# A tuned two-block transformer kernel on one core: TensorE's tile slots brought to 768 instructions each, with 256-column passes and waits that are already met

## Chip, cores and metric

The kernel runs on one core of a Trainium2 chip. The metric is the device time of one execution in microseconds (us); lower is better. In the text PE is TensorE (PEld its weight loads), DVE is VectorE, ACT is ScalarE, POOL is GpSimd and SP is SyncE, which issues the DMAs.

## The reference, cut to what matters

The input is four sequences of 512 tokens with 128 features. Two adaptive-norm blocks follow. The first has a 16-head ALiBi attention and a mixture of eight experts. The second has a 4-head attention with a memory term, and then a small transformer of six layers, which is where the change lies:

```python
for i in range(DEPTH):            # DEPTH = 6, x: 4 x 512 x 128
    x = attn_layer(shift_tokens(x), Wqkv[i], q_scale[i], k_scale[i], Wo[i]) + x
    x = ffn_layer(shift_tokens(x), ln_g[i], ln_b[i], W1[i], b1[i], W2[i], b2[i]) + x
# attn_layer: qkv = x @ Wqkv (128 x 3072); q, k normalised and rotated;
#   16 heads of 64, windows of 32 queries on 64 keys; softmax; @ V; @ Wo (1024 x 128)
# ffn_layer: layernorm; a, gate = split(xn @ W1 + b1); (a * gelu(gate)) @ W2 + b2
```

## The kernel before, in words

Each engine has its own hand-written instruction stream, and semaphores join them. Until about 690 us the kernel computes the first block and the attention of the second. Then comes the **tile stage**: `run_slots` (L443) calls the engine's `slot` function 96 times, for 6 layers x 4 sequences x 4 tiles of 128 tokens (t = 0 to 3). The number of a slot is g. A slot is software-pipelined: it projects its own tile g, and does the window attention of g-1 and g-2 and parts of the feed-forward network of sequences before it. `drain` (L1285) finishes what is left.

On TensorE a slot (`slot`, L1127) runs in this order, which is the order of the code:

- `queries(0)`: a projection (`project`, L1036) onto 512 of the 3072 columns. It has three passes in float32r, since x and W are split into high and low parts: high x high, high x low, low x high. They accumulate in `pj`.
- `wo_quarter` (L1179): the output projection of one tile, 8 float32 products of 128x128 on `wo`. The trace shows two passes for each float32 product.
- for t = 3 a norm's transposes (`norm_in`), then `queries(1)`, the second projection; for t = 3 also `ff_down` (L1187).
- `probs` (L1152): 8 transposes of softmax weights; then `project(.., 2)`.
- `values_(0)` (L1161): 32 small products of 64x32 on `slab` (V2) into `oo`; then `project(.., 3)`.
- `turn_k` (L1145): 16 transposes; then `values_(1)`, 32 more small products, and `project(.., 4)`.
- `window_scores(.., 0)` (L1085): 32 small products into `sc`.
- `out_` (L1172): 16 transposes of the attention's result (`tr<-ident,slab`). They wait for DVE's `weighted`.
- for t < 3 `ff_up` (L1117): one third of the first feed-forward product, 6 passes of float32r in two accumulation groups. For t = 3 `norm_back` instead, 4 transposes.
- `window_scores(.., 1)`, `turn_q` (16 transposes) and `project(.., 5)`.

Each product is two instructions in TensorE's stream, a weight load (LDWEIGHTS) and a MATMUL. A float32 product that is no transposition is four, because of its two passes. Further semaphore waits than the one that an instruction carries itself are instructions of their own, and one of these holds up to two waits. Counted so, a slot has 713 to 717 instructions for t < 3, and 733 or 734 for t = 3. The whole stream has 76,612: twice 37,572, and 1,468 wait instructions. No instruction of this kernel is in a loop; the stream is straight.

Of the kernel before, what the change touches and what calls it, by code (L numbers as in the profile page):

```python
# [15 lines left out]
P = 128  # L16
B = 4
S = 512
# [78 lines left out]
        self.eng.wait_ge(self.sem, self.base + self.n)  # L97

PTR = 6
NMAX = 2 * H0 * T
# [7 lines left out]
def build(nc, ins, out):  # L110
    ctx = ExitStack()
    with ctx:
# [52 lines left out]
        w1_lo = nc.alloc_sbuf_tensor_at("w1_lo", [P, 2 * DI], F32R, offset=w1_at)  # L165
# [11 lines left out]
        hB_hi = nc.alloc_sbuf_tensor_at("hB_hi", [P, S], F32R, offset=xcur_at + 4 * S)  # L177
        hT_at = here()
        hT = sb("hT", [P, 2, S])
        hB_lo = nc.alloc_sbuf_tensor_at("hB_lo", [P, S], F32R, offset=hT_at)  # L180
        xs_lo = nc.alloc_sbuf_tensor_at("xs_lo", [P, S], F32R, offset=hT_at + 4 * S)
# [4 lines left out]
        xs_hi = sb("xs_hi", [P, S], F32R)  # L186
# [85 lines left out]
        def rows(b):  # L272
# [15 lines left out]
        spare = a.take(3, INNER)  # L288
# [6 lines left out]
        w1_hi = nc.alloc_sbuf_tensor_at("w1_hi", [P, 2 * DI], F32R, offset=arena_at + 4 * a.at)  # L295
# [15 lines left out]
        pj = ctx.enter_context(nc.psum_tensor("pj", [P, 2, S], F32))  # L311
# [9 lines left out]
        ld_const = sem("ld_const")  # L321
        ld_late = sem("ld_late")
# [34 lines left out]
        pj_mm, sq_ev, rot_ev, ss_ok, qk_rdy, v_cp = (  # L357
            sem("pj_mm"), sem("sq_ev"), sem("rot_ev"), sem("ss_ok"), sem("qk_rdy"), sem("v_cp"))
# [8 lines left out]
        ld_w1, w1_h, w1_l, hb_h, hb_l = sem("ld_w1"), sem("w1_h"), sem("w1_l"), sem("hb_h"), sem("hb_l")  # L367
# [247 lines left out]
        n_const, n_mid, n_late = (16 * N_CONST.count(k) for k in range(3))  # L615
# [12 lines left out]
        def _(pe):  # L628
            def mm(o, l, r, start=True, stop=True, **k):
                return nc.tensor.matmul(o, l, r, start=start, stop=stop, **k)  # L630
# [35 lines left out]
            for g in range(2):  # L666
                for k in range(4):
                    last = tp(tr[:, g, k * P:(k + 1) * P], wnat[:, 4 * g + k, :])
# [367 lines left out]
            def project(g, t, c):  # L1036

                low_, high_ = W_LO[g // (T * B) % 2], W_HI[g // (T * B) % 2]
                if c < 2:
                    wait(pe, v_cp, g * 2 - 1 + c)  # L1040
                else:
                    pe.wait_ge(rot_ev, g * 4 + c - 1)
                x_, w_ = slice(t * P, (t + 1) * P), slice(c % 2 * S, (c % 2 + 1) * S)
                k = c // 2
                mm(pj[:, c % 2], xs_hi[:, x_], high_[k][:, w_], stop=False)
                mm(pj[:, c % 2], xs_hi[:, x_], low_[:, k, w_], start=False, stop=False)
                mm(pj[:, c % 2], xs_lo[:, x_], high_[k][:, w_], start=False).then_inc(pj_mm, 1)

            def turn_rows(rows, done, ready, first, second):

# [66 lines left out]
            def ff_up(m, k, bank):  # L1117
                w = CH[k][1]
                for half, o in ((1, DI + CH[k][0]), (0, CH[k][0])):
                    mm(bank[0:w, half], w1_hi[:, o:o + w], hB_hi[:, :], stop=False)  # L1120
                    mm(bank[0:w, half], w1_lo[:, o:o + w], hB_hi[:, :], start=False, stop=False)
                    if half:
                        pe.wait_ge(hb_l, m + 1)
                    last = mm(bank[0:w, half], w1_hi[:, o:o + w], hB_lo[:, :], start=False)
                last.then_inc(w1_mm, 1)

            def slot(s_):  # L1127
                l, b, t, n, g = s_.l, s_.b, s_.t, s_.n, s_.g
                new, c_, d_, m1, m2 = s_.new, s_.c_, s_.d_, s_.m1, s_.m2
                n2, t2 = (n, t - 2) if t >= 2 else (n - 1, t + 2)  # L1130
                weighted_ = min(g - 2, NTILE)

                def queries(c):
                    if c == 0 and t < 2:
                        pe.wait_ge(xs_l, n * 2 + t + 1)
                    project(g, t, c)
# [42 lines left out]
                def wo_quarter(m, i):  # L1179
                    pe.wait_ge(o_cp, (m * T + i + 1) * 2)  # L1180
                    tok, held = slice(i * P, (i + 1) * P), slice(i % 2 * P, (i % 2 + 1) * P)
                    for p_ in range(PAIRS):
                        last = mm(oo[:, 1, tok], wo[:, p_, :], oT[:, p_, held], start=(p_ == 0),
                                  stop=(p_ == PAIRS - 1))
                    last.then_inc(wo_mm, 1)
# [11 lines left out]
                if b == 0 and t == 0:  # L1197
                    pe.wait_ge(wl_ok[0], l + 1)
                queries(0)
                if s_.mw is not None:  # L1200
                    if b == 0 and t == 3:
                        pe.wait_ge(ld_wo, (l + 1) * G * 16)
                    if 1 <= t < 3 and m2 is not None:
                        pe.wait_ge(up_cp, m2 * 4 + 2 * t - 1)
                    if t == 3 and m2 is not None:
                        pe.wait_ge(gelu_ev, gated(m2, 2))
                    wait(pe, on_ok, g * 2 - 4)
                    wo_quarter(s_.mw, s_.iw)
                if t == 3 and m1 is not None:
                    pe.wait_ge(t_sub, g - 1)  # L1210
                    pe.wait_ge(xs_part, m1 * T + T)
                    norm_in(LNB, LNB_BANKS[0], xsF)
                queries(1)
                if g > 0:
                    crossing(g, 1)
                if g == 1:
# [1327 lines left out]
```

## Time and profile before

| | us |
|---|---|
| median of 3 runs | 2113.81 (2111.32 to 2116.18) |
| the profiled execution's own time | 2119.18 |
| its span in the trace | 2117.4 |
| PE busy / DVE busy / ACT busy / POOL busy | 1943.4 / 1821.4 / 1546.8 / 1290.5 |
| tile stage, slots 8 to 94 (87 slots) | 1357.18 |

The span is what the trace covers; the execution's own time has some 1.8 us around it. "Busy" is the time in which an engine has an instruction at work. The rows further down are from this one execution. In a timeline row "x64" is a number of MATMULs in a row (two for each of the 32 small products), and "[1.09 <-issue]" is idle time ahead of the row and what ended it: the engine that was waited for, or "issue" where the profile sees nothing that was waited for. In the rows 64*32 is the loaded weight, and a small product's output is 32x64.

### The profile page before, as it was taken

To read this page: it belongs to the slowest core of one execution; us is meant where nothing else is said; L and a number is where in the kernel's file an instruction comes from. 1 tells how busy PE (TensorE), PEld (TensorE's weight loads), DVE (VectorE), ACT (ScalarE), POOL (GpSimd) and SP (SyncE) were. 2 spreads that over 40 slices of the span, in tenths; PEclk is the share of its full clock that TensorE was granted. 3 is DMA by queue.
4 is the path that set the end of the run, shared out by engine and by line. 5 is a ranking of instruction groups with operands and counts; after the bars stand their busy time and mean duration, and the time that the engine had idled before them with its cause. 6 is when DMAs were issued, how large, how long until landed. Compare 5 with 4: busy or idle time off the path is not lost.

```text
span 2117.4 us, 89360 instructions
## 1 busy us (share of the span) xinstructions
PE 1943.4 (92%) x37572; PEld 1442.3 (68%) x37572; DVE 1821.4 (86%) x3995; ACT 1546.8 (73%) x3028; POOL 1290.5 (61%) x1551
## 2 busy tenths in 40 slices
PE   6888899987788999999999999999999999999996
PEld 4666664455566777777777777777777777777774
DVE  6788775577798999999899999999999998998994
ACT  4777763355576877888788887888878878777873
POOL 1111110000378888788787888878888887777771
PEclk9999999998899999999999999999999999999998
DMA  5000000100232322332333323333233332222321
GB/s 117 2 2 2 2 32 31 61 1 1 58 86 70 79 68 70 93 84 67 78 83 78 87 65 77 86 89 79 67 81 83 87 75 63 73 75 73 77 63 41
DMA packets 99377, 132.62 MB, mean 63 GB/s; under 512 B 29052, under 2 KB 44034, under 8 KB 98978
## 3 DMA queue, kind: packets, MB, share of 16 engines
q1 hardware_dynamic: 98978, 126.90, 23.6%
q8 instruction: 299, 4.90, 1.0%
q14 instruction: 100, 0.82, 0.1%
HBM read 28.20 MB, written 1.11 MB: 14 GB/s over the span
## 4 chain that ended last, share of the span: by engine, by line
PE 48%; DVE 23%; ACT 10%; issue 9%; SPq 5%; POOL 3%; DMA 2%; DVEq 0%; POOLq 0%; ACTq 0%
PE pj L630 15%; PE oo L630 15%; ACT arena L1961 7%; PE sc L630 6%; PE tr L1057 5%; DVE arena L1764 4%; DVE arena L1766 4%; SPq L555 3%; PE tr L633 3%; DMA slab<-arena 2%; DVE bv L1772 2%; DVE arena L1521 2%; DVE small L1795 1%; DVE xn L1353 1%; ACT L1965 1%
## 5 line engine op out<-in xcount | busy, mean ns | idle before, releaser
L1961 ACT ACTIVATE arena<-tr 128x512 f32<-128x512 f32 (+3 forms) x894 | 458.8, 562 | 100.0 <-PE tr L633 51.3
L2397 POOL TENSOR_TENSOR arena<-arena 128x1024 f32<-128x1024 f32 x192 | 457.4, 2382 | 91.3 <-DVE arena L1766 87.5
L1961 ACT ACTIVATE arena<-pj 128x512 f32<-128x512 f32 x576 | 332.5, 599 | 150.9 <-PE pj L630 96.1
L2415 POOL TENSOR_TENSOR arena<-arena,small 128x1024 f32<-128x1024 f32 x192 | 365.6, 1904 | 28.1 <-POOL small L2408 0.9
L1961 ACT ACTIVATE arena<-arena 128x1024 f32<-128x1024 f32 (+4 forms) x446 | 304.6, 693 | 87.6 <-DVE arena L1521 74.0
L1772 DVE TENSOR_REDUCE bv<-arena 128x8 f32<-128x512 f32 x384 | 252.7, 679 | 2.9
L630 PE MATMUL oo<-slab,arena 64*32 64x64 f32 (+1 forms) x12416 | 232.7, 229 | 10.5 <-issue 9.7
L2364 POOL TENSOR_SCALAR rstd<-mv 128x4 f32<-128x4 f32 x40 | 11.4, 284 | 364.5 <-DVE mv L1347 364.4
L633 PE MATMUL tr<-ident,arena 128*128 128x128 f32 x1346 | 206.4, 280 | 19.4 <-DMA beta<-in_L_attn_betas 9.9
L630 PEld LDWEIGHTS oo<-slab,arena 64*32 64x32 f32 (+1 forms) x12416 | 160.8, 106 | 80.0 <-issue 44.4
L633 PEld LDWEIGHTS tr<-ident,arena 128*128 128x128 f32 x1346 | 163.3, 143 | 58.3 <-issue 23.9
L630 PEld LDWEIGHTS sc<-arena 64*32 64x32 f32 x12288 | 136.1, 105 | 87.6 <-issue 71.9
L630 PEld LDWEIGHTS oo<-arena,wo 128*128 128x128 f32 x1504 | 183.6, 193 | 8.7 <-DMA wo<-in_L_ffn_Wo 0.3
L630 PE MATMUL sc<-arena 64*32 64x64 f32 x12288 | 171.7, 224 | 18.4 <-issue 17.5
L630 PE MATMUL oo<-arena,wo 128*128 128x128 f32 x1504 | 184.4, 276 | 0.0
L1785 DVE TENSOR_REDUCE small<-sc 128x16 f32<-128x1024 f32 x96 | 117.3, 1222 | 46.9 <-PE sc L630 46.9
L1764 DVE TENSOR_TENSOR arena<-pj,rtab 128x512 f32<-128x512 f32 x192 | 131.3, 684 | 29.3 <-ACT arena L1961 27.3
L1057 PEld LDWEIGHTS tr<-ident,arena 64*128 64x128 f32 x3072 | 111.3, 139 | 63.0 <-issue 42.1
L1057 PE MATMUL tr<-ident,arena 64*128 64x64 f32 x3072 | 138.0, 229 | 16.6 <-ACT arena L1961 9.3
L1764 DVE TENSOR_TENSOR arena<-pj,wT 128x512 f32<-128x512 f32 x192 | 131.2, 684 | 22.0 <-ACT arena L1961 19.3
L1809 DVE TENSOR_TENSOR slab<-oo,small 128x512 f32<-128x512 f32 x192 | 123.7, 686 | 12.1 <-PE oo L630 8.7
L1766 DVE TENSOR_TENSOR arena<-pj,wT 128x512 f32<-128x512 f32 x192 | 130.8, 681 | 0.0
(340 smaller groups left out, 4465.0 us busy)
## 6 DMA issues: line engine op xcount, KB each, us to landing
slab<-arena SPq DMA_DIRECT2D x576, 128.0 KB
slab<-arena SPq DMA_DIRECT2D x336, 64.0 KB
arena<-gate_mem SPq DMA_DIRECT2D x24, 256.0 KB, 4.4
wqkv<-in_L_ffn_Wqkv SPq DMA_DIRECT2D x36, 128.0 KB, 2.5
arena<-in_L_ffn_Wqkv SPq DMA_DIRECT2D x36, 128.0 KB, 2.3
wo<-in_L_ffn_Wo SPq DMA_DIRECT2D x24, 128.0 KB, 2.5
w<-in_L_ffn_W SPq DMA_DIRECT2D x6, 341.0 KB, 3.6
YT<-in_L_attn_x SPq DMA_DIRECT2D x4, 256.0 KB, 3.9
```

The lines of the kernel that those rows point to most:

```text
L555: sp.dma_start(V2[u * DL:(u + 1) * DL, t % 2, w, :], Vt[(w - 1) * WIN:(w + 1) * WIN, t % 2, f]).then_inc(v2_in[t % 2], 16)
L630: return nc.tensor.matmul(o, l, r, start=start, stop=stop, **k)
L633: return nc.tensor.transpose(o, i, ident[0:i.shape[0], 0:i.shape[0]])
L1057: last = nc.tensor.transpose(tr[:, u, pr * DL:(pr + 1) * DL], rows(r, pr), ident[r, r])
L1764: v.tensor_tensor(ra[:, t % 2, k, co].rearrange("p (h u d) -> p h u d", u=2, d=DL // 2), src, tc_.unsqueeze(1).broadcast_to(wide), ALU.mult)
L1766: v.tensor_tensor(rb[:, k, co].rearrange("p (h u d) -> p h u d", u=2, d=DL // 2), src[:, :, ::-1, :], ts_.unsqueeze(1).broadcast_to(wide), ...
L1772: v.tensor_reduce(ss[:, k, hf * PAIRS:(hf + 1) * PAIRS, 0], sq[:, c % 2].rearrange("p (h d) -> p h d", d=DL), AX.X, ALU.add).then_inc(ss_o ...
L1785: v.tensor_reduce(mx, s_v, AX.X, ALU.max).then_inc(mx_ok, 1)
L1809: v.tensor_tensor(On.rearrange("p (a u d) -> p u a d", u=2, d=DL)[:, :, a_], oo[:, :, :].rearrange("p u (a d) -> p u a d", d=DL)[:, :, a_] ...
L1961: return nc.scalar.activation(o, i, f, **k)
L2397: p_.tensor_tensor(r_, r_, rb[:, k, :], ALU.add).then_inc(sum_ok, 1)
L2415: p_.tensor_tensor(r3, r3, rs[:, k, :].unsqueeze(2).broadcast_to([P, HL, DL]), ALU.mult).then_inc(qk_rdy, 1)
```

## The change

Only TensorE's stream changes, and only in the tile stage. The streams of the other engines hold the same instructions in the same order. Three things are done:

1. `project` runs its three passes over 256 columns instead of 512 for c = 0, 1, 2 and 5, twice over. That is 12 more load-and-product pairs in a slot. `ff_up` does the same for its tokens, 6 more pairs in each slot with t < 3, and its first group waits for `hb_l` in both halves.
2. `spread_out` adds wait instructions on `ld_const` and `ld_late`, semaphores of the loads at the kernel's start. The same stream has already waited for both values before the tile stage. A slot gets 17, 19, 19 or 10 of them (t = 0 to 3), in three groups: behind `queries(0)`, behind `wo_quarter` and behind `queries(1)`.
3. Slots 0 to 7 have numbers of their own (0, 0, 0, 0, 8, 43, 43, 24), which sets where in the stream the count of 256 begins anew inside the slots that follow.

```diff
+SPARE_AT = (17, 19, 19, 10)
+SPARE = {0: 0, 1: 0, 2: 0, 3: 0, 4: 8, 5: 43, 6: 43, 7: 24}
...
-                mm(pj[:, c % 2], xs_hi[:, x_], high_[k][:, w_], stop=False)
-                mm(pj[:, c % 2], xs_hi[:, x_], low_[:, k, w_], start=False, stop=False)
-                mm(pj[:, c % 2], xs_lo[:, x_], high_[k][:, w_], start=False).then_inc(pj_mm, 1)
+                x_, k, n = slice(t * P, (t + 1) * P), c // 2, S // (2 if c in (0, 1, 2, 5) else 1)
+                parts = [(slice(o, o + n), slice(c % 2 * S + o, c % 2 * S + o + n)) for o in range(0, S, n)]
+                for o_, w_ in parts:
+                    mm(pj[:, c % 2, o_], xs_hi[:, x_], high_[k][:, w_], stop=False)
+                    mm(pj[:, c % 2, o_], xs_hi[:, x_], low_[:, k, w_], start=False, stop=False)
+                    last = mm(pj[:, c % 2, o_], xs_lo[:, x_], high_[k][:, w_], start=False)
+                last.then_inc(pj_mm, 1)
...
+                    tok = [slice(u * S // 2, (u + 1) * S // 2) for u in range(2)]
+                    for u in tok:
+                        mm(bank[0:w, half, u], w1_hi[:, o:o + w], hB_hi[:, u], stop=False)
+                        mm(bank[0:w, half, u], w1_lo[:, o:o + w], hB_hi[:, u], start=False, stop=False)
+                        if half:
+                            pe.wait_ge(hb_l, m + 1)
+                        last = mm(bank[0:w, half, u], w1_hi[:, o:o + w], hB_lo[:, u], start=False)
...
+            def spread_out(n):
+                for _ in range(n):
+                    pe.wait_ge(ld_const, n_const)
+                    pe.wait_ge(ld_late, n_late)
...
+                spare = SPARE.get(g, SPARE_AT[t])
...
                 queries(0)
+                spread_out(spare // 3)
...
                     wo_quarter(s_.mw, s_.iw)
+                spread_out(spare // 3)
...
                 queries(1)
+                spread_out(spare - spare // 3 * 2)
```

Every slot from g = 8 on then has 768 instructions on TensorE (one of 767 or 770 stands where a layer's weights change), and the stream 81,328 in all.

The start of a slot with t = 0 on PE, in the program before, from `queries(0)` to `queries(1)` (`wq_hi` is the high part of the query weights, `w_lo` the low part, the suffix B the second buffer):

```order
L630 MATMUL pj<-wq_hiB,xs_hi 128x512 [waits v_cp,xs_l]
L630 MATMUL pj<-w_loB,xs_hi 128x512
L630 MATMUL pj<-wq_hiB,xs_lo 128x512
L630 MATMUL oo<-arena,wo 128x128 [waits o_cp,on_ok]
L630 MATMUL oo<-arena,wo 128x128 x7
L630 MATMUL pj<-wq_hiB,xs_hi 128x512 [waits v_cp]
L630 MATMUL pj<-w_loB,xs_hi 128x512
L630 MATMUL pj<-wq_hiB,xs_lo 128x512
```

The same place in the changed program:

```order
L633 MATMUL pj<-wq_hiB,xs_hi 128x256 [waits v_cp,xs_l]
L633 MATMUL pj<-w_loB,xs_hi 128x256
L633 MATMUL pj<-wq_hiB,xs_lo 128x256
L633 MATMUL pj<-wq_hiB,xs_hi 128x256
L633 MATMUL pj<-w_loB,xs_hi 128x256
L633 MATMUL pj<-wq_hiB,xs_lo 128x256
L633 MATMUL oo<-arena,wo 128x128 [waits ld_const,ld_late,on_ok,o_cp]
L633 MATMUL oo<-arena,wo 128x128 x7
L633 MATMUL pj<-wq_hiB,xs_hi 128x256 [waits ld_const,ld_late,v_cp]
```

Each projection has six products instead of three, and the added waits stand between it and `wo_quarter`, and again before the next projection. The places of the other products have not moved.

The feed-forward part of a slot with t < 3 on PE, before; the row behind it is the second half of the window scores:

```order
L630 MATMUL oo<-hB_hi,w_hi 128x512 [waits on_ok,hb_h]
L630 MATMUL oo<-hB_hi,w_lo 128x512
L630 MATMUL oo<-hB_lo,w_hi 128x512 [waits hb_l]
L630 MATMUL oo<-hB_hi,w_hi 128x512
L630 MATMUL oo<-hB_hi,w_lo 128x512
L630 MATMUL oo<-hB_lo,w_hi 128x512
L630 MATMUL sc<-arena 32x64 x32
```

And the first six of its twelve rows in the changed program (six more without waits follow, then the same row of window scores):

```order
L633 MATMUL oo<-hB_hi,w_hi 128x256 [waits on_ok,hb_h,w1_l]
L633 MATMUL oo<-hB_hi,w_lo 128x256
L633 MATMUL oo<-hB_lo,w_hi 128x256 [waits hb_l]
L633 MATMUL oo<-hB_hi,w_hi 128x256
L633 MATMUL oo<-hB_hi,w_lo 128x256
L633 MATMUL oo<-hB_lo,w_hi 128x256 [waits hb_l]
```

Twelve products of half the width stand in the place of six.

## Rows read from the trace of the kernel before

**Rows 1.** The page: TensorE's busy line, and the queue that brings instructions.

```profile
PE 1943.4 (92%) x37572; PEld 1442.3 (68%) x37572; DVE 1821.4 (86%) x3995; ACT 1546.8 (73%) x3028; POOL 1290.5 (61%) x1551
...
q8 instruction: 299, 4.90, 1.0%
```

**Rows 2.** Windows: slots 8 to 94 together, then three single slots (columns in the first row).

```profile
core 0: us, PE busy (x) PEld busy (x) DVE busy (x) ACT busy (x) POOL busy (x), PEclk, DMA share, GB/s
689.79:2046.97 1357.18, 1304.21 (x30794) 1011.40 (x30792) 1250.43 (x2296) 1102.40 (x2081) 1101.18 (x1302) 1.00 0.31 77
1066.50:1081.03 14.53, 14.40 (x354) 11.31 (x353) 13.99 (x25) 12.84 (x26) 11.43 (x15) 1.00 0.41 100
...
1468.93:1483.46 14.53, 14.53 (x353) 11.36 (x352) 13.51 (x24) 13.20 (x23) 12.16 (x16) 1.00 0.32 77
1111.66:1128.74 17.08, 16.48 (x362) 12.37 (x360) 16.71 (x37) 12.45 (x26) 12.56 (x16) 1.00 0.28 72
```

**Rows 3.** Waits of PE from 700 to 2060 us: total, times, longest.

```profile
PE sc L630 <- issue: 12.9, 17, 1.4
PE tr L1057 <- DVE slab L1809: 8.9, 18, 1.4
PE tr L1057 <- ACT arena L1961: 8.4, 13, 1.3
```

**Rows 4.** Timeline of PE in the first half of a slot's window scores.

```profile
1011.03 0.64 PE L630 MATMUL sc<-arena 64*32 64x64 f32 x38
1012.76 0.43 PE L630 MATMUL sc<-arena 64*32 64x64 f32 x26 [1.09 <-issue]
```

**Rows 5.** Windows from one such break to two later ones (columns as in rows 2).

```profile
1012.70:1028.98 16.28, 14.65 (x378) 11.77 (x378) 14.11 (x26) 12.08 (x25) 13.45 (x16) 1.00 0.25 60
1012.70:1090.76 78.06, 74.09 (x1765) 57.83 (x1764) 70.57 (x130) 62.32 (x120) 63.68 (x75) 1.00 0.29 72
```

**Rows 6.** Windows of five single stretches of 256 instructions.

```profile
1102.94:1106.56 3.62, 2.53 (x133) 1.86 (x130) 3.58 (x8) 3.56 (x8) 3.23 (x9) 1.00 0.52 146
...
1007.80:1012.75 4.95, 3.87 (x130) 2.72 (x125) 4.92 (x9) 3.95 (x8) 3.45 (x6) 1.00 0.51 123
996.93:1000.33 3.40, 2.88 (x141) 2.29 (x138) 3.33 (x8) 1.90 (x5) 3.25 (x4) 1.00 0.02 5
1071.20:1075.14 3.94, 3.86 (x148) 2.71 (x134) 3.90 (x8) 3.33 (x7) 2.39 (x1) 1.00 0.65 156
1075.14:1078.84 3.70, 3.65 (x137) 2.82 (x141) 3.67 (x7) 3.08 (x7) 3.10 (x6) 1.00 0.09 22
```

**Rows 7.** Timeline of PE at the window scores of a slot with t = 3.

```profile
996.81 0.86 PE L630 MATMUL sc<-arena 64*32 64x64 f32 x64
998.14 0.97 PE L1057 MATMUL tr<-ident,slab 64*128 64x64 f32 x16 [0.47 <-DVE slab L1809]
...
999.63 1.02 PE L630 MATMUL sc<-arena 64*32 64x64 f32 x64
```

**Rows 8.** Timeline of PE: 512-column passes of `ff_up`, and `wo_quarter`.

```profile
1887.38 0.39 PE L630 MATMUL oo<-hB_hi,w_hi 128*128 128x512 f32 x1
1887.61 0.40 PE L630 MATMUL oo<-hB_hi,w_lo 128*128 128x512 f32 x1
...
1892.31 1.95 PE L630 MATMUL oo<-arena,wo 128*128 128x128 f32 x16
1894.02 0.47 PE L630 MATMUL pj<-wq_hiB,xs_hi 128*128 128x512 f32 x1
```

**Rows 9.** Timeline of PE in the first block: float32r passes of 256 and 384 columns.

```profile
185.80 0.37 PE L630 MATMUL pj<-Kst,Qm 128*128 128x256 f32 x1
186.00 0.38 PE L633 MATMUL tr<-ident,arena 128*128 128x128 f32 x2
186.14 0.42 PE L630 MATMUL sc<-Kst,Qm 128*128 128x384 f32 x1
186.41 0.49 PE L633 MATMUL tr<-ident,arena 128*128 128x128 f32 x3
```

More of the change, by code:

```diff
@@ L1042, in project @@
                     pe.wait_ge(rot_ev, g * 4 + c - 1)
-                x_, w_ = slice(t * P, (t + 1) * P), slice(c % 2 * S, (c % 2 + 1) * S)
-                k = c // 2
-                mm(pj[:, c % 2], xs_hi[:, x_], high_[k][:, w_], stop=False)
-                mm(pj[:, c % 2], xs_hi[:, x_], low_[:, k, w_], start=False, stop=False)
-                mm(pj[:, c % 2], xs_lo[:, x_], high_[k][:, w_], start=False).then_inc(pj_mm, 1)
+                x_, k, n = slice(t * P, (t + 1) * P), c // 2, S // (2 if c in (0, 1, 2, 5) else 1)
[5 more added lines that the diff above has]
+                last.then_inc(pj_mm, 1)
             def turn_rows(rows, done, ready, first, second):
@@ L1119, in ff_up @@
                 for half, o in ((1, DI + CH[k][0]), (0, CH[k][0])):
[L1120 to L1124, printed above, removed]
+                    tok = [slice(u * S // 2, (u + 1) * S // 2) for u in range(2)]
[5 more added lines that the diff above has]
+                        last = mm(bank[0:w, half, u], w1_hi[:, o:o + w], hB_lo[:, u], start=False)
                 last.then_inc(w1_mm, 1)
+            def spread_out(n):
+                for _ in range(n):
+                    pe.wait_ge(ld_const, n_const)
+                    pe.wait_ge(ld_late, n_late)
             def slot(s_):
```

## The prediction, as it was put on record

> **What bounds the kernel now.** I read the page first. PE is the busiest engine at 92%, with DVE behind it at 86% [rows 1]. Then I cut out the tile stage, the only part that the change touches: in 87 slots of it PE is busy for 1304.2 of 1357.2 us, at a granted clock of 1.00, and DVE for 1250.4 [rows 2]. So PE is the bound there, and all of its idle time is 53.0 us. A slot takes 1357.18 / 87 = 15.60 us.
>
> Third, the waits. The three longest groups of them stand ahead of the small products and transposes, and the first is put down to "issue": nothing that the profile sees was waited for [rows 3]. The timeline shows one of these breaks. It falls inside 64 equal passes of window scores, behind the 38th, and lasts 1.09 us; no semaphore stands there [rows 4].
>
> Fourth, the counts. From this break to the next one at 1028.98 there are 378 products, so 756 instructions, and 12 waits by the program: 768, three times 256. To a break inside another group of scores at 1090.76 there are 1765 products, so 3530, and 54 waits: 3584, 14 times 256 [rows 5]. And the queue that brings instructions moved 299 packets of 4.90 MB [rows 1], 16.4 KB each, for the 76,612 instructions of PE's stream: 256.2 to a packet. So PE's instructions come in **pieces of 256**, and the breaks are at the starts of pieces.
>
> Last, how long a piece needs. I counted on from 1012.76 and read stretches of 256 instructions. One that holds only small products, one projection and scores has 2.53 us of work and took 3.62; another with 3.87 took 4.95. Two others with nearly 4 us of work, 3.94 and 3.70, took what their work takes [rows 6]. My reading: the next piece is called for only around the start of the one before, and a piece can't take less than some 3.4 to 4 us, now and then 5. A piece with a projection or two lasts longer and hides this; one of mostly small products doesn't. Slots have 713 to 734 instructions, so the starts of pieces wander through them, and every few slots a short piece comes up.
>
> One text speaks against this reading. The Trainium skill, "Runtime: NRT & Kernel Launch", section "Instruction fetch mechanics", also has blocks of 16 KiB or 256 instructions, but says that the fetch is "hidden by the ~20-cyc/instr NX issue floor". By that the breaks would have another cause and placing the starts would save nothing; that is the third rival below. The break of rows 4 speaks against it.
>
> **The change, part by part.** The sum is made against the profiled execution, 2119.18 us (span 2117.4), 5.4 us over the median.
>
> *Removed: wandering starts.* Undisturbed slots with t < 3 take 14.53 us, and with t = 3 17.08 [rows 2]. Four of them take 3 x 14.53 + 17.08 = 60.67, or 15.17 a slot. What short pieces cost now is 15.60 - 15.17 = 0.43 a slot, times 87: **37 us**. The undisturbed slots hold the real waits for DVE and ACT; those remain.
>
> *Added: fixed starts.* With 768 in each slot, a slot always has three starts at the same places. Counted on through the changed stream, which is the same up to the tile stage, they are:
> - in `values_(0)` (19th of its 32 products; 15th for t = 3),
> - early in the first half of the window scores (8th; 4th for t = 3),
> - late in the second half (25th).
>
> Piece A, from values to scores, holds two projections, a turn and 45 small products. Its like in the trace is the stretch at 1071.20: 3.94 us for 3.86 of work [rows 6], 0.05 lost at the most likely.
>
> Piece B, from scores to scores, holds `out_` and for t < 3 `ff_up`. Its like is the stretch at 1075.14: 3.70, with 3.65 of work [rows 6]. In the changed stream `ff_up` has 12 instructions more, so B ends some 3 products sooner, at about 3.55 of work. Against a need of 3.4 to 4 that loses between 0 and 0.45; I take 0.1, near the low end, since the stretch at 1075.14 went by in 3.70.
>
> For t = 3 B has no `ff_up`. From 996.9 it holds the rest of the scores, 0.47 of waiting for DVE, 16 transposes, 4 more and 25 small products, some 2.9 us in all; the second half of the scores then took 1.02 where 0.86 is the rule, a start of a piece with little delay [rows 7]. The stretch from 996.93, which begins and ends near the same products, took 3.40 [rows 6]. So this loses from 0.16, the delay in rows 7, to 1.1 at a need of 4; I take 0.45, to the 3.4 of the like stretch.
>
> Piece C is the rest, 7 us or more, and loses nothing. Four slots lose 3 x (0.05 + 0.1) + 0.05 + 0.45 = 0.95 us; 87 / 4 x 0.95 = **21 us** come back. The gain by placement is 37 - 21 = 16.
>
> *Added: more passes.* There are 12 more in each slot and 6 more for t < 3, so 66 in four slots. A 512-column pass follows the last after 0.23 [rows 8]. A 256-column pass was followed after 0.20 by the transposes, a 384-column pass after 0.27 [rows 9], so 128 columns are worth about 0.06 to 0.07, and four times 0.0575 is the 0.23. The pass costs by its columns, with hardly a fixed part, if the load of its weights is hidden. Behind 128 columns in float32, 16 loads and passes took 1.71 us from start to start, 0.107 each [rows 8], so a load is done within 0.107 and fits behind a pass of 0.115. I take 2 ns for each added pass: 66 x 0.002 x 87 / 4 = **3 us**. Bounds: nothing, since the columns are the same; and 5 ns, since rounding hides that much, 7 us. That the load isn't hidden is excluded by the 0.107.
>
> *Added: met waits.* 65 in four slots, 1430 in all. They are queued behind a projection (0.69 us of passes) or `wo_quarter` (1.71), ahead of work that isn't waited for soonest, and PE's queue takes what is issued ahead. Rows 8 show `wo_quarter` with two waits ahead of it and the projection behind it, one more wait, with no break. So **0**. If that cover were gone, as after a projection that was itself late, each would cost what it takes to issue; no row has that. Slots 5 and 6 have 14 or 15 in a group, and there I allow 1 us once. Upper bound: 0.1 us a slot, 9 us.
>
> DVE's order is not changed. It needs 1250.4 of the 1357.2 us [rows 2], so it would become the bound only at 106 us saved.
>
> Sum: 2119.2 - 37 + 21 + 3 + 1 = 2107, which is 12 less; against the median of 2113.8 that is **2102**.
>
> **The rivals.**
>
> *Short pieces are slower than I take them (slower).* If a piece that begins in the scores always needs 4.0 us, each B loses 0.45 for t < 3 and 1.1 for t = 3: 4 x 0.05 + 3 x 0.45 + 1.1 = 2.65 in four slots. 58 us come back, and with 4 for passes and waits the kernel takes 2113.8 - 37 + 58 + 4 = 2139. The point from which it decides: 33 us may come back, 1.5 in four slots, 1.3 of it in B; 3 x (need - 3.55) + (need - 2.9) = 1.3 gives a need of 3.7 in every B. For: 4.95. Against: 3.62, 3.40, and 3.70 with hardly a break [rows 6]. Chance 0.17, mostly with a need little over that point, 2118 to 2130.
>
> *All is hidden (much faster).* B lasts long enough for t < 3, and for t = 3 its start falls into the wait for DVE. Then 37 is gained and 4 lost: 2081. For: 0.16 of delay in rows 7. Against: the spread in rows 6. Chance 0.13.
>
> *The breaks are no fetches (no change).* Then only passes and waits are added: 2114 + 4 = 2118, or with waits that cost nothing 2114. For: two of the three longest groups are put down to DVE and ACT, 17.3 us [rows 3]. Against: breaks 256 apart. The same time results if PE, no longer held at starts, waits for DVE's `weighted` instead. Chance 0.15. (The section of the Trainium skill named above would make this the likeliest.)
>
> **How the numbers follow.** The forecast case has 0.55: 2102, from 2090 to 2113. A measurement of this kernel can tell 0.2%, 4.2 us, from no change. Faster (under 2109.6): 0.50 of the forecast case and 0.13, 0.63. Same: 0.05 and 0.15, 0.20. Slower: 0.17. The range for 8 in 10 leaves out the far ends on both sides: 2084 to 2121.
>
> **What would show it.** In the profile after: 318 packets in the instruction queue; slots of 768 instructions whose breaks all stand behind the same product, in scores or not at all; slots with t < 3 near 14.7 and nearly equal; t = 3 at 17.4 to 17.7; passes of 256 columns 0.115 to 0.12 apart; no idle time ahead of `wo_quarter` and `queries(1)`. It is wrong if t < 3 slots take over 15.1, if breaks stand in the second half of scores in most slots, or if 256-column passes are 0.13 or more apart.

## The result, and the profile after

The changed kernel takes 2099.1 us (median of 6 runs, 2091.14 to 2105.65). The kernel before took 2112.57 beside it on the same chip (6 runs, 2105.12 to 2116.18). The ratio is **0.994**, 95% interval 0.9914 to 0.9968. The forecast was 2102. The profiled execution took 2105.65, with a span of 2103.9.

The page of the changed kernel, first part and queues, against [rows 1]:

```profile
PE 1957.8 (93%) x39156; PEld 1558.3 (74%) x39156; DVE 1820.7 (87%) x3995; ACT 1547.0 (74%) x3028; POOL 1290.6 (61%) x1551
...
q8 instruction: 317, 5.19, 1.0%
```

Windows of the changed kernel (columns as in rows 2): slots 8 to 94, then three single slots, of which the second has t = 3, then slots 0 to 7, slot 7 alone, and all that follows slot 94:

```profile
697.38:2031.72 1334.34, 1309.04 (x32234) 1109.49 (x32233) 1249.73 (x2296) 1102.33 (x2082) 1100.54 (x1302) 1.00 0.31 79
1498.09:1512.66 14.57, 14.53 (x372) 12.67 (x371) 14.02 (x24) 12.66 (x25) 11.50 (x14) 1.00 0.31 75
1541.81:1559.01 17.20, 16.54 (x375) 13.11 (x373) 16.61 (x38) 11.89 (x26) 13.84 (x17) 1.00 0.26 64
1189.70:1205.46 15.76, 14.71 (x372) 12.70 (x371) 14.56 (x24) 12.15 (x25) 14.21 (x16) 1.00 0.32 78
564.55:697.38 132.83, 106.82 (x2401) 89.45 (x2399) 113.08 (x211) 82.76 (x164) 95.31 (x116) 0.88 0.27 69
678.15:697.38 19.23, 17.34 (x368) 14.89 (x367) 15.59 (x35) 13.01 (x26) 13.27 (x16) 0.76 0.25 64
2031.72:2103.90 72.18, 55.73 (x957) 44.38 (x955) 42.73 (x78) 29.35 (x51) 19.60 (x24) 0.86 0.17 45
```

The same of the kernel before, where they did not stand in rows 2: slots 0 to 7, slot 7, and what follows slot 94:

```profile
563.37:689.79 126.42, 100.22 (x2303) 76.86 (x2302) 112.94 (x211) 82.26 (x164) 94.53 (x116) 0.95 0.28 72
672.36:689.79 17.43, 14.07 (x355) 11.20 (x354) 16.22 (x36) 13.24 (x26) 12.80 (x17) 1.00 0.28 71
2046.97:2117.40 70.43, 52.90 (x911) 38.02 (x909) 42.31 (x78) 29.58 (x51) 19.60 (x24) 0.92 0.18 47
```

Waits of PE from 700 us on in the changed kernel, against [rows 3]:

```profile
PE tr L1062 <- DVE slab L1826: 10.0, 21, 0.5
PE tr L1062 <- ACT arena L1978: 7.8, 8, 1.1
...
PE sc L633 <- issue: 0.7, 3, 0.3
```

Rows 3 show one group that ends in "issue". The kernel before has three more of them in the same stretch, which the changed kernel doesn't have at all:

```profile
PE oo L630 <- issue: 7.7, 15, 0.9
PE tr L1057 <- issue: 4.6, 6, 1.5
...
PE pj L630 <- issue: 1.4, 3, 0.5
```

What there is to see:

- **The waits that nothing explained are gone.** "issue" was 26.6 us in all, 12.9 of it ahead of the scores, and is 0.7. The waits for DVE and ACT, which are real, stayed (8.9 and 8.4 before, 10.0 and 7.8 now). PE's idle time in the 87 slots fell from 53.0 to 1334.34 - 1309.04 = 25.3 us.
- **Most slots are now the same.** They take 14.57 us, or 17.20 for t = 3; the means over the windows are 14.76, 14.60, 14.85 and 17.23 (t = 0 to 3). The slot at 1189.70 is one of the few that don't, and its break is a real wait, the first row below.
- **The time went into two places that the prediction left out.** The 87 slots gained 22.8 us, but slots 0 to 7 lost 6.4 and the part behind slot 94 lost 1.8. In both the granted clock is lower: 0.88 for 0.95, and 0.86 for 0.92. In slots 0 to 7 PE's busy time rose by 106.82 - 100.22 = 6.6 us, and its idle time stayed at 26.

Timeline of PE in the changed kernel: the break in the slot at 1189.70, two 256-column passes at 2.4 GHz, and two in slot 2:

```profile
1203.41 0.71 PE L1062 MATMUL tr<-ident,arena 64*128 64x64 f32 x16 [1.01 <-ACT arena L1978]
...
1500.23 0.29 PE L633 MATMUL pj<-wq_hiB,xs_lo 128*128 128x256 f32 x1
1500.35 0.28 PE L633 MATMUL pj<-wq_hiB,xs_hi 128*128 128x256 f32 x1
...
601.91 0.41 PE L633 MATMUL pj<-w_lo,xs_hi 128*128 128x256 f32 x1
602.12 0.41 PE L633 MATMUL pj<-wq_hi,xs_lo 128*128 128x256 f32 x1
```

A pass is followed after 0.12 us in a full slot and after 0.21 in slot 2, whose granted clock is 0.81. The second is the lower level, 1.2 GHz.

| stretch | before | after | difference |
|---|---|---|---|
| up to slot 0 | 563.37 | 564.55 | +1.2 |
| slots 0 to 7 | 126.42 | 132.83 | +6.4 |
| slots 8 to 94 | 1357.18 | 1334.34 | -22.8 |
| behind slot 94 | 70.43 | 72.18 | +1.8 |
| span | 2117.4 | 2103.9 | -13.5 |

Each column is one execution. A second profile of the changed kernel (e11 below) has 563.16, 132.60, 1337.89 and 72.35, so that slots 8 to 94 gain 19.3 us there, and the first row shows no difference.

### The profile page after: what moved, and what is told of

Read it like the earlier page. It is cut to its first block, busy times and chain, and to the rows that moved or that the text cites. A ratio compares the mean times of both kernels' runs of the same rounds, so it can differ in the third digit from the quotient of the medians.

```text
span 2103.9 us, 94076 instructions
## 1 busy us (share of the span) xinstructions
PE 1957.8 (93%) x39156; PEld 1558.3 (74%) x39156; DVE 1820.7 (87%) x3995; ACT 1547.0 (74%) x3028; POOL 1290.6 (61%) x1551
## 4 chain that ended last, share of the span: by engine, by line
PE 57%; DVE 19%; ACT 10%; issue 7%; SPq 3%; POOL 2%; DMA 2%; DVEq 0%; POOLq 0%; ACTq 0%
PE pj L633 19%; PE oo L633 19%; ACT arena L1978 7%; PE tr L1062 6%; PE sc L633 6%; PE tr L636 4%; DVE arena L1781 3%; DVE arena L1783 2%; ACT L1982 2%; SPq L558 2%; DVE xn L1370 2%; DVE arena L1538 2%; DMA slab<-arena 1%; PE oo L636 1%; DVE small L1812 1%
## 5 line engine op out<-in xcount | busy, mean ns | idle before, releaser
L633 PE MATMUL oo<-slab,arena 64*32 64x64 f32 (+1 forms) x12416 | 227.7, 229 | 2.5 <-issue 1.8
L633 PEld LDWEIGHTS oo<-arena,wo 128*128 128x128 f32 x1504 | 177.4, 193 | 0.5 <-issue 0.2
L633 PE MATMUL pj<-w_lo,xs_hi 128*128 128x256 f32 (+1 forms) x480 | 148.8, 310 | 0.0
L1781 DVE TENSOR_TENSOR arena<-pj,wT 128x512 f32<-128x512 f32 x192 | 131.1, 683 | 19.4 <-ACT arena L1978 18.3
L633 PE MATMUL pj<-w_loB,xs_hi 128*128 128x256 f32 (+1 forms) x480 | 145.8, 304 | 0.0
```

Of the source, the lines that this page charges most:

```text
L1781: v.tensor_tensor(ra[:, t % 2, k, co].rearrange("p (h u d) -> p h u d", u=2, d=DL // 2), src, tc_.unsqueeze(1).broadcast_to(wide), ALU.mult)
```

## The experiments

All diffs are against the changed kernel. **Where the starts stand** is given as a number x: the first start of a slot stands x instructions behind the last pass of `queries(0)`, the others 256 and 512 further on. In the change x is 168. The wait of `values_(0)` for `v2_*` and `pt_cp`, at which PE's sequencer really stands in each slot (for 1.1 to 3 us, an estimate from the timelines), is instruction 91 (t = 0), 93 (t = 1 and 2) or 107 (t = 3) by the same count. The numbers for slots 4 to 7 set x for the rest of the stage. Slot times by t are means over the slots' windows unless a single slot is named.

| kernel | x | waits a slot | slots 8 to 94 | ratio to before (95%) |
|---|---|---|---|---|
| the change | 168 | 10 to 19 | 1334.3 | 0.9941 (0.9914 to 0.9968) |
| e11_change_again | 168 | 10 to 19 | 1337.9 | 0.9937 (0.9918 to 0.9956) |
| e3_early_shift | 168 | 10 to 19 | 1339.8 | 0.9936 (0.9916 to 0.9956) |
| e7_starts_earlier | 153 | 10 to 19 | 1336.5 | 0.9943 (0.9925 to 0.9962) |
| e9_late_passes | 158 | 10 to 19 | 1339.0 | 0.9933 (0.9910 to 0.9956) |
| e6_starts_later | 217 | 10 to 19 | 1345.8 | 1.0010 (0.9993 to 1.0027) |
| e4_passes_only | wanders | 0 | 1361.9 | 1.0024 (1.0011 to 1.0037) |
| e10_one_group | 168 | 10 to 19, together | 1391.7 | 1.0169 (1.0133 to 1.0204) |
| e1_other_starts | 8 | 10 to 19 | 1397.2 | 1.0220 (1.0194 to 1.0247) |
| e2_best_starts | 64 | 10 to 19 | 1393.2 | 1.0240 (1.0212 to 1.0268) |
| e8_wait_47_in | 44 | 10 to 19 | 1388.7 | 1.0273 (1.0251 to 1.0295) |
| e5_waits_only | 192 | 34 to 55 | 1448.8 | 1.0470 (1.0444 to 1.0497) |

### e1_other_starts

```diff
-SPARE = {0: 0, 1: 0, 2: 0, 3: 0, 4: 8, 5: 43, 6: 43, 7: 24}
+SPARE = {0: 0, 1: 0, 2: 0, 3: 0, 4: 6, 5: 6, 6: 5, 7: 5}
```

> The changed kernel with 22 instead of 118 added waits in slots 4 to 7, all else the same. Each slot from g = 8 on still has 768 instructions of the same kinds in the same order, but the piece of 256 begins 160 instructions earlier in it: in wo_quarter, in turn_k and in out_. Placement theory: read off the changed kernel's own timeline, the stretch between the second and third start has about 2.3 us of work where some 3.6 are needed, so four slots lose 4.8 us and 88 slots about 105; less 4 us for the fewer waits: 2099 + 100 = 2199, ratio to the kernel before 1.035 to 1.055, slots with t < 3 near 15.8. Rival (the narrower passes and the waits do it, wherever pieces begin): no slower than the change, 2095 to 2100, ratio 0.992 to 0.995. Rival (DVE and ACT set the time): the same 2095 to 2100.

It took 2163.36 us, ratio 1.022. Slots 8 to 94 in the windows, and the largest group of PE's waits from 700 us on:

```profile
691.49:2088.67 1397.18, 1318.95 (x32234) 1118.76 (x32233) 1251.03 (x2296) 1109.24 (x2083) 1104.51 (x1303) 0.99 0.30 75
...
PE sc L633 <- issue: 69.3, 75, 1.6
```

The same instructions, in the same order from slot 8 on; only the place in them where a piece of 256 begins is another. The group that went from 12.9 to 0.7 in the change is now 69.3: a break or two in nearly every slot with t < 3, and none to speak of for t = 3, which took 17.19. So **the place of the starts alone is worth 63 us between the best and a bad choice**, and the breaks are the starts of pieces. Counted through the streams, all 75 breaks over 0.4 us that end in "issue" in this stretch of e1 open a piece of 256; so do all 31 such breaks of the kernel before, and of the 25 breaks over 0.4 us that it owes to DVE or ACT one does. The 63 us are some 0.6 of the loss that was expected.

### e2_best_starts

```diff
-SPARE = {0: 0, 1: 0, 2: 0, 3: 0, 4: 8, 5: 43, 6: 43, 7: 24}
+SPARE = {0: 0, 1: 0, 2: 0, 3: 0}
...
+            for _ in range(314):
+                pe.wait_ge(ld_x[0], 16)
```

The loop stands at the start of PE's program and gives 157 instructions, two waits in each.

> The changed kernel with its slots' pieces beginning 104 instructions earlier in the slot than in the change (about 64 behind the end of queries(0)), and the 118 waits of slots 4 to 7 replaced by the usual 17, 19, 19, 10; the rest of the shift, 157 waits, stands at the start of the program, where PE waits for the first loads for about 10 us anyway. By the changed kernel's timeline every piece then holds 4.1 us of work or more. Placement theory: no piece breaks at all, slots 14.56 and 17.2, which is 15.22 on average against 15.34 (10 us), and slots 4 to 7 give back 5 to 6 us: 2084 to 2088, ratio 0.985 to 0.990. If starts are not what costs: 2093, by the slots 4 to 7 alone, or 2099 if the early waits cost what those did.

A clear miss: 2167.55 us, ratio 1.024, although by their work no piece is short. Two things went wrong. The first is in the timeline of PE at the start of the program, e2:

```profile
20.99 1.94 PE L636 MATMUL tr<-ident,arena 128*128 128x128 f32 x8 [20.99 <-issue]
```

The kernel before:

```profile
9.87 1.97 PE L633 MATMUL tr<-ident,arena 128*128 128x128 f32 x8 [9.87 <-DMA beta<-in_L_attn_betas]
```

157 waits that are already met hold PE up by 11.1 us. The first of them is taken at some 4.1, when the load of x has landed, so each takes (20.99 - 4.1) / 157 = 0.108 us. e8, with 20 more of them in the same place, needs no such reading: it starts at 23.21, which is 0.111 us for each of the 20.

```profile
23.21 1.94 PE L636 MATMUL tr<-ident,arena 128*128 128x128 f32 x8 [23.21 <-issue]
```

 **A met wait isn't free; it takes PE's sequencer some 0.11 us.**

The second is in every slot. Timeline of PE in e2, a slot with t = 3 (from 1519.10), and under it ACT, whose first copy of `tr` is what `values_(0)` waits for:

```profile
1528.72 0.41 PE L633 MATMUL oo<-slab,arena 64*32 64x64 f32 x21
1530.09 0.68 PE L633 MATMUL oo<-slab,arena 64*32 64x64 f32 x43 [0.95 <-issue]
...
1525.36 1.09 ACT L1980 ACTIVATE arena<-tr 128x512 f32<-128x512 f32 x2 [1.42 <-PE tr L636]
```

PE has done the piece's last product at 1529.14 and goes on at 1530.09. The piece had begun at 1522.05, behind the last pass of `queries(1)`: 8.0 us, where the longest of rows 6 took 4.95. The DMA view tells why. From 1522.00 to 1527.20 the queues moved this:

```profile
DMA packets 589, 0.92 MB, mean 177 GB/s; under 512 B 139, under 2 KB 139, under 8 KB 589
q1 hardware_dynamic: 589, 0.92, 69.7%
```

And from 1527.20 to 1527.40:

```profile
q8 instruction: 1, 0.02, 47.3%
```

In the first 5.2 us of the piece no packet of instructions moves at all. The packet with the next piece comes at 1527.2, 1.2 us after the wait of `values_(0)` was met (1526.0), and 2.8 us later PE goes on. Of the 22 slots of e2 with t = 3, 15 show this, with the packet 1.1 to 1.7 us after the wait was met; in the other 7 the packet came 3.2 to 3.3 us before it, which stays unexplained. So the next piece isn't called for at the start of the one before, as the prediction had it, but some way into it, and a wait that really holds the sequencer in between delays the call by all that it takes. In e2 this wait is 27 or 29 instructions behind a start (43 for t = 3); in the change 179 or 181 (195).

### e3_early_shift

```diff
-SPARE = {0: 0, 1: 0, 2: 0, 3: 0, 4: 8, 5: 43, 6: 43, 7: 24}
+SPARE = {0: 0, 1: 0, 2: 0, 3: 0}
...
+            for _ in range(106):
+                pe.wait_ge(ld_x[0], 16)
```

> The change with the starts of pieces exactly where the change has them, but reached by 53 waits at the start of the program and the usual 65 in slots 4 to 7. All theories: equal to the change but for slots 4 to 7, which are 5 to 6 us shorter: 2093 to 2094, ratio 0.990 to 0.992. If the 86 waits in slots 5 and 6 are free, as the prediction had it to within 1 us: 2098, ratio 0.994.

2104.76 us, ratio 0.9936: not to be told from the change, and not the 0.990 to 0.992 that was expected. The 53 waits stand where PE waits for a load anyway (its first product starts at 10.12 instead of 9.87). Slots 0 to 7 took 130.8 us, 2 less than in the change, and not the 126.4 of before: so it isn't mainly the 53 extra waits in slots 4 to 7 that slow the filling.

### e4_passes_only

```diff
             def spread_out(n):
+                n = 0
 
                 for _ in range(n):
```

> The narrower passes without any added wait: 749 or 751 instructions in a slot, 758 for t = 3, so the starts wander again, by 18 or so a slot. Placement theory: about as slow as the kernel before, since wandering starts cost 30 to 45 us in 88 slots, plus 3 us for the passes: 2112 to 2120, ratio 1.000 to 1.004. Rival (the narrower passes themselves give the gain): 2099, ratio 0.994.

2123.09 us, ratio 1.0024. Slots 8 to 94:

```profile
693.72:2055.57 1361.85, 1314.11 (x32234) 1112.55 (x32233) 1250.40 (x2296) 1105.21 (x2083) 1102.46 (x1303) 1.00 0.31 77
```

The 256-column passes bring nothing by themselves. PE is busy for 9.9 us more than before and the stretch is 4.7 longer, and the starts wander as before: "issue" is 28.6 us in all, for 26.6 before. The gain is the placement's.

### e5_waits_only

```diff
-SPARE_AT = (17, 19, 19, 10)
-SPARE = {0: 0, 1: 0, 2: 0, 3: 0, 4: 8, 5: 43, 6: 43, 7: 24}
+SPARE_AT = (53, 55, 55, 34)
+SPARE = {0: 0, 1: 0, 2: 0, 3: 0, 4: 9, 5: 9, 6: 9, 7: 9}
...
-                x_, k, n = slice(t * P, (t + 1) * P), c // 2, S // (2 if c in (0, 1, 2, 5) else 1)
+                x_, k, n = slice(t * P, (t + 1) * P), c // 2, S
...
-                    tok = [slice(u * S // 2, (u + 1) * S // 2) for u in range(2)]
+                    tok = [slice(0, S)]
```

> The change without its 256-column passes: the products are those of the kernel before, and the 768 of a slot are filled up with met waits alone (53, 55, 55, 34 a slot; 9 in each of slots 4 to 7), so that the pieces begin behind the same products as in the change. If it is the places of the starts that save the time and a met wait costs nothing, slots with t < 3 take 14.5 to 14.7, and the ratio to before is 0.988 to 0.996, like the change's 0.994. If the shorter passes had a part in the gain, it is 0.996 to 1.003. If a met wait costs 3 ns or more, the 197 a period of four slots add 0.6 us and more, and the ratio is 1.000 and up.

2213.32 us, ratio 1.047, the worst of all. The largest waits of PE in the tile stage:

```profile
PE tr L636 <- issue: 76.4, 61, 1.3
PE oo L633 <- issue: 20.6, 21, 1.1
```

And the timeline of PE in a slot with t = 1, at two of the three groups of 18 or 19 waits:

```profile
1506.09 0.39 PE L633 MATMUL pj<-wq_hiB,xs_lo 128*128 128x512 f32 x1
1507.40 2.02 PE L633 MATMUL oo<-arena,wo 128*128 128x128 f32 x16 [0.93 <-issue]
...
1510.00 0.39 PE L633 MATMUL pj<-wq_hiB,xs_lo 128*128 128x512 f32 x1
1511.64 1.06 PE L636 MATMUL tr<-ident,arena 128*128 128x128 f32 x8 [1.25 <-issue]
```

The starts are quiet: scores lose 4.9 us to "issue" in the whole stage. The time is lost at the waits, in gaps of 0.9 to 1.3 us behind each projection. 18 waits at 0.11 are 2 us, and what PE still has queued covers the rest. So the third answer of the expectation holds, and the "3 ns" in it was far too low a bound: 132 waits more in four slots cost 114.5 us in 87, or 40 ns each on the average. With so many waits this run can't show what the starts alone would bring without the narrower passes.

### e6_starts_later and e7_starts_earlier

```diff
-SPARE = {0: 0, 1: 0, 2: 0, 3: 0, 4: 8, 5: 43, 6: 43, 7: 24}
+SPARE = {0: 0, 1: 0, 2: 0, 3: 0, 4: 17, 5: 17, 6: 17, 7: 18}
```

> The change with all three starts 49 instructions later in each slot (17, 17, 17, 18 waits in slots 4 to 7), so that the wait of values_(0) for DVE stands some 130 instructions behind a start and the scores are begun at other places. If only the work between two starts counts (need 3.6 us), no piece is short at all, t = 3 takes under 17.2 and the ratio is 0.985 to 0.992. If a piece is called for only when PE's sequencer is some 40 to 56 instructions into the one before, the delays of those first instructions count too, every slot breaks once by 0.5 to 1.1 us, and the ratio is 1.005 to 1.025.

```diff
-SPARE = {0: 0, 1: 0, 2: 0, 3: 0, 4: 8, 5: 43, 6: 43, 7: 24}
+SPARE = {0: 0, 1: 0, 2: 0, 3: 0, 4: 12, 5: 48, 6: 48, 7: 25}
```

> The change with all three starts 15 instructions earlier (12, 48, 48, 25 waits in slots 4 to 7). Both theories, the one by the work between starts and the one by the call 40 to 56 instructions in, leave at most 0.6 us lost in four slots: ratio 0.989 to 0.997, slots with t < 3 near 14.6. If starts in values_(0) are good only at the very place of the change, it is over 1.0.

e7 came out as both theories had it: 2102.19 us, ratio 0.9943, t < 3 at 14.66 to 14.89. The place has some 15 instructions of room on that side. e6 gave 2116.37, ratio 1.001, between the two expectations. Its waits of PE:

```profile
PE sc L633 <- issue: 8.8, 13, 1.1
...
PE tr L1062 <- issue: 7.2, 14, 1.0
```

It breaks in some slots and not in others, 27 times in 87 slots: t = 3 takes 17.63, where the change has 17.23, t = 2 15.0, t = 0 and 1 14.74 and 14.61. A theory that counts only the work between two starts is refuted, since by it e6 is the best place of all. The other had the direction and not the size: at least 1.005.

### e8_wait_47_in

```diff
-SPARE = {0: 0, 1: 0, 2: 0, 3: 0, 4: 8, 5: 43, 6: 43, 7: 24}
+SPARE = {0: 0, 1: 0, 2: 0, 3: 0}
...
+            for _ in range(354):
+                pe.wait_ge(ld_x[0], 16)
```

> As e2_best_starts, with 20 more waits at the start of the program: the starts are 20 instructions earlier, and the wait of values_(0) for DVE stands 47 instructions into its piece instead of 27 (62 and 42 for t = 3). By the work between the starts this is worse than e2: some 1.2 us lost in four slots where that theory gives e2 nothing; e2 lost 3.2. If the call for the next piece is made about 40 instructions in, the wait no longer holds it up: under 1.5 us lost in four slots, slots with t < 3 at 14.6 to 15.0, ratio 0.995 to 1.010. If it is made about 56 in, it does: 2.5 to 3.5 lost, ratio 1.018 to 1.030.

2172.04 us, ratio 1.027. In e8 the wait is 47 instructions behind a start for t = 0, 49 for t = 1 and 2, and 63 for t = 3. The slots took 16.16, then 15.09 and 15.52, then 17.13. Against the change's undisturbed 14.57 and 17.20 that is 1.6 us lost, then 0.5 and 0.95, then nothing. The ratio and these 3 us in four slots are what was expected if the call is made about 56 in; but that t = 3 loses nothing at 63, and that t = 1 and 2 lose less than t = 0, narrows it from both sides. In e2, with the wait 43 in, t = 3 took 17.71. The windows of the same slot with t = 3, e2:

```profile
1519.10:1537.30 18.20, 16.42 (x374) 13.13 (x373) 17.35 (x38) 13.12 (x26) 12.88 (x19) 1.00 0.25 61
```

And e8, with its `values_(1)` in the timeline, in which e2 broke for 0.95 us:

```profile
1520.72:1537.82 17.10, 16.56 (x374) 13.18 (x373) 16.66 (x38) 12.43 (x26) 12.27 (x16) 1.00 0.26 65
...
1530.34 0.86 PE L633 MATMUL oo<-slab,arena 64*32 64x64 f32 x64
1531.27 0.50 PE L633 MATMUL pj<-wv_hiB,xs_hi 128*128 128x512 f32 x1
```

In e8 this piece began at 1522.7, and the packet of instructions comes between 1523.30 and 1523.50:

```profile
q8 instruction: 1, 0.02, 38.3%
```

That is 0.7 us after the start and 4 us before the wait of `values_(0)` is met. So the same real wait of some 3 us holds up the call in most slots when it stands 43 instructions in (15 of 22), and in none of 22 when it stands 63 in. At 47 all 17 packets come 1.1 us or more after the release; at 49 they come from 0.4 us before it to 1.6 after. **The call is made when PE's sequencer is about 50 instructions into a piece.** From the packet to the next piece's first instruction it then took 2.8 us in e2; where a piece of e1 opens with a break of over 0.3 us it is 2.3 to 3.1. A piece needs its first 50 instructions, some 0.7 us up to the packet where nothing holds them, and about 2.8: 3.5 us, the 3.4 to 4 of the prediction.

### e9_late_passes

```diff
-SPARE = {0: 0, 1: 0, 2: 0, 3: 0, 4: 8, 5: 43, 6: 43, 7: 24}
+SPARE = {0: 0, 1: 0, 2: 0, 3: 0, 4: 16, 5: 16, 6: 16, 7: 16}
...
-                x_, k, n = slice(t * P, (t + 1) * P), c // 2, S // (2 if c in (0, 1, 2, 5) else 1)
+                x_, k, n = slice(t * P, (t + 1) * P), c // 2, S // (2 if g > 7 and c in (0, 1, 2, 5) else 1)
...
-            def ff_up(m, k, bank):
+            def ff_up(m, k, bank, cuts=2):
...
-                    tok = [slice(u * S // 2, (u + 1) * S // 2) for u in range(2)]
+                    tok = [slice(u * S // cuts, (u + 1) * S // cuts) for u in range(cuts)]
...
-                    ff_up(m2, t, oo)
+                    ff_up(m2, t, oo, 2 if g > 7 else 1)
```

> The change with the 256-column passes left out of slots 0 to 7, and 16 waits in each of slots 4 to 7: the filling of the stage is the kernel before's but for 64 waits, and from slot 8 on the starts are 10 instructions earlier than in the change, inside the stretch (15 earlier to the change's own places) that two runs showed to be equally good. If the filling was slowed by the passes' moved starts alone, slots 0 to 7 take 126 to 128.5 us instead of 132.8, slots 8 to 94 1332 to 1340, and the ratio to before is 0.989 to 0.993, some 4 to 6 us under the change. If the filling was slow for the waits that were met there, nothing comes back, and the ratio is 0.993 to 0.996.

Slots 0 to 7 in the windows of e9:

```profile
563.76:690.30 126.54, 100.63 (x2306) 76.75 (x2305) 112.06 (x211) 81.82 (x164) 93.66 (x115) 0.95 0.28 73
```

The filling is the kernel before's again, with its granted clock of 0.95 (the change: 132.83 at 0.88). Beside e11 on the same chip it took 2103.51 us against 2106.41, 2.9 less, less than the 4 to 6 that were expected, and these runs can't tell it from nothing; the spans of their profiled executions are 2100.7 and 2106.0. e9 beats the kernel before (0.991 to 0.9956) and isn't shown to beat the change.

The other runs bear out that it is the passes. In the ten profiles with them in slots 0 to 7 (the change, e1 to e4, e6 to e8, e10 and e11) these slots took 128.2 to 132.8 us at a granted clock of 0.88 to 0.92. In the three without (before, e5, e9) they took 126.4 to 126.7 at 0.95. e4, which has the passes and no added wait, took 129.9: so some 3.5 us of the change's 6.4 come with the passes alone.

### e10_one_group

```diff
                 queries(0)
-                spread_out(spare // 3)
+                spread_out(0 if g > 7 else spare // 3)
...
                     wo_quarter(s_.mw, s_.iw)
-                spread_out(spare // 3)
+                spread_out(0 if g > 7 else spare // 3)
...
-                spread_out(spare - spare // 3 * 2)
+                spread_out(spare if g > 7 else spare - spare // 3 * 2)
```

> The change with the same number of waits and the same starts, but from slot 8 on all waits of a slot (17, 19, 19, 10) in one group behind queries(1), instead of a third each behind queries(0), wo_quarter and queries(1). If a met wait costs nothing wherever it stands, the ratio is the change's 0.992 to 0.996. If each takes PE's sequencer some 60 ns and only what PE's queue holds of earlier work hides them (e5's groups of 17 or 18 showed 1.1 to 1.4 us each), a group of 19 behind 12 passes shows 0.5 to 1.2 us a slot for t < 3: slots with t < 3 at 15.1 to 15.7, ratio 1.008 to 1.030.

2157.99 us, ratio 1.017, t < 3 at 15.46 to 15.68. The waits of PE, and the timeline behind `queries(1)`, where now 19 stand together:

```profile
PE tr L636 <- issue: 57.2, 64, 1.0
...
1483.51 0.28 PE L633 MATMUL pj<-wq_hiB,xs_lo 128*128 128x256 f32 x1
1484.81 1.06 PE L636 MATMUL tr<-ident,arena 128*128 128x128 f32 x8 [1.01 <-issue]
```

The number of waits, of passes and every start are the change's. Only that the waits of a slot stand together costs 57.2 us. Since the change's groups of 5 to 7 show no gap, PE has queued some 0.7 to 1 us of work that covers the sequencer: 19 x 0.108 = 2.05, less the 1.01 that showed.

### e11_change_again

> The changed kernel itself, for a comparison on the same chip and against the same runs of before: ratio 0.991 to 0.997, slots 0 to 7 at 131 to 134 us. If the gain were the luck of one chip it would be within 0.998 to 1.002.

2106.41 us, ratio 0.9937 (0.9918 to 0.9956), with slots 0 to 7 at 132.6. The gain repeats on another chip than that of e1 to e4 and of e5 to e8.

## Why the prediction was right, and where it wasn't

The forecast of 2102 stands beside 2099.1. By its own steps:

- **What bounds the kernel, and pieces of 256.** Right. 317 packets came where 318 were named. e1 leaves no other reading: the same stream gives 0.7 or 69.3 us of "issue" by where the pieces begin, and every such break opens a piece. The third rival (breaks are no fetches) is refuted. The Trainium skill, "Runtime: NRT & Kernel Launch", section "Instruction fetch mechanics", has the next block fetched while the current one runs, which the packets show; that this hides it isn't so here, by the 69.3 us in e1.
- **Removed, 37 us.** Too much: this term took all that slots had over the best kind. "issue" was 26.6 us of it, more than rows 3 show; the rest, some 10 us, are real waits of single slots for DVE or ACT, which no placement removes. Slots of the best kind did become the rule. Four of them now take 3 x 14.57 + 17.20 = 60.91, and 87 of this kind (66 with t < 3, 21 with t = 3) 1322.8.
- **Fixed starts return 21 us.** This term failed. By the prediction's own 60.67 for four slots, 87 slots take 1319.6, and they took 14.8 us more. Of this 4.8 are the passes (below) and only 0.7 is "issue", which is all that stands in the place of the 21; the other 9 lie in a few slots that wait for ACT or DVE, as the one at 1189.70 (PE's waits for ACT alone are 7.8 us in 8 places), and were in the 37 by mistake. The need of 3.4 to 4 was about right, but B for t < 3 lasts long enough, and for t = 3 the breaks that were to bring it to 17.4 to 17.7 don't show: 17.20. In the slot from 1541.81 both halves of the scores run through:

```profile
1553.34 0.86 PE L633 MATMUL sc<-arena 64*32 64x64 f32 x64
1554.68 0.97 PE L1062 MATMUL tr<-ident,slab 64*128 64x64 f32 x16 [0.48 <-DVE slab L1826]
...
1556.16 0.86 PE L633 MATMUL sc<-arena 64*32 64x64 f32 x64
```

From the 4th product of the first to the 25th of the second that is 3.3 us, DVE's 0.48 among them, and it was enough. So in slots 8 to 94 the second rival (all is hidden, 0.13) is nearer to what happened. No start falls into the wait for DVE, as it had it for t = 3; the wait lies inside the piece and lengthens it. Its 2081 failed on the 9 us and on what follows.
- **Left out: the filling and the end.** The sum treated only slots 8 to 94. Slots 0 to 7, the start and the end gave back 6.4 + 1.2 + 1.8 = 9.4 us, most of it where PE's granted clock was lower. So that the total of -12 (-13.5 in the spans) came out so near was luck, by two errors of opposite sign: for slots 8 to 94 the terms gave -13 and it was -22.8, 10 too pessimistic, and around them they were 9 too optimistic.
- **Passes, 3 us.** PE's busy time rose by 1309.04 - 1304.21 = 4.8 us for 66 x 87 / 4 = 1436 added passes, 3.4 ns each, where 2 was taken and 5 was the bound. It is not sharp: e11, the same kernel, has 1312.44, which is 5.7 ns each, and the undisturbed slots with t < 3 went from 14.53 to 14.57 for 18 passes, 2.2 ns each. The Trainium skill, "TensorE: Matmul & The Clock Gate", section "Wait — 56ns, not 53.3ns?", gives a product a fixed 2.5 ns at 2.4 GHz; the 2.2 to 5.7 of these traces are of that size. In the filling, with the lower granted clock, 6.6 us more of PE's busy time went with 98 more passes, which was not foreseen.
- **Met waits, 0.** Right for the change as written, and for a reason that wasn't known: groups of 5 to 7 are just covered. "What it takes to issue", which no row had, is 0.11 us. The upper bound of 0.1 us a slot was far too low for any other grouping (e10: 57 us, e5: 114).
- **What was called for when.** The prediction had the next piece called for "only around the start of the one before". It is about 50 instructions in, as e2 and e8 show, with 7 slots of e2 left over. This didn't change the sum, since in the change nothing holds the sequencer in those 50.
- **The first rival** (a need over 3.7 in every B, 2139) didn't happen: no break stands in the scores of the change to speak of.

Open: why the granted clock in the filling is lower with the 256-column passes, and which slots it strikes (slot 7 has 0.76 in the change's profile and 1.00 in e11's); how e6 loses in a third of its slots and not in the others; and why the call wasn't held in 7 of e2's slots. The 1.2 us ahead of slot 0 are not in e11's profile.

## What to carry to other kernels

In a long straight stream on TensorE, count instructions: where "issue" stands ahead of small products at places 256 instructions apart, a piece is too short, and the cure is to have its start placed so that the stretch to the next one lasts over 3.5 us, and no wait that really waits stands in the first 50 instructions behind it. Pad with work that PE would do anyway (a pass cut in two costs some 2 to 6 ns at the full clock), and with met waits only in groups of 5 or so behind dense products, since each takes the sequencer 0.11 us. And sum such a change over the filling and the draining of the pipeline too, where PE's granted clock was lower here, and lower still with the added passes.

## What the runs showed of the hardware that was not expected

- A wait instruction that is already met takes PE's sequencer 0.108 us (157 of them, e2), or 0.111 (the 20 more of e8). A group of 19 behind a projection showed 1.01 us, groups of 5 to 7 none.
- The next 256 instructions are called for when PE's sequencer is about 50 into the current ones: a wait of some 3 us delayed the packet at 43 instructions in 15 of 22 slots (packet 1.2 us after its release in the one shown) and not at 63 (packet 4 us before it). From the packet to the first instruction of the new piece it was 2.8 us in e2, and 2.3 to 3.1 where a piece of e1 opens with a break.
- The same stream from slot 8 on, with the same instructions, takes from 1334 to 1397 us by where the pieces begin.
- With 98 passes and loads of 256 columns more in slots 0 to 7, the mean granted clock there was 0.88 instead of 0.95 and 6.4 us were lost (0.88 to 0.92 and 1.8 to 6.4 us over ten profiles); without them both came back (e9).
